# Score maxima of two attention heads taken in pairs, in two row groups of the matrix engine

## The chip, the cores and the metric

The kernel runs on one core of one Trainium2 chip. The metric is the device time of one execution in microseconds (us). Five engines work side by side, each with a queue of its own: PE (TensorE, the matrix engine), DVE (VectorE), ACT (ScalarE), POOL (GpSimd) and SP (SyncE, which issues most transfers). They meet at semaphores.

## The reference

One transformer layer in float32: causal attention over 4 sequences of 2048 tokens with 4 heads of 64, a residual and a layer norm, then a routed feed-forward part with 32 experts and 16 adapters, another residual and a layer norm.

```python
q = split_heads(x @ wq.T) * hd ** -0.25
k = split_heads(x @ wk.T) * hd ** -0.25
v = split_heads(x @ wv.T)
q, k = (_rope(q), _rope(k))
energy = jnp.einsum('bhtd,bhld->bhtl', q, k) + mask
attn = jax.nn.softmax(energy, axis=-1)
out = jnp.einsum('bhtl,bhld->bhtd', attn, v)
```

The change is in the attention stage alone. The softmax needs a shift for each query row that is near that row's largest score; which one exactly does not alter the result.

## The kernel before

**Tiles and stages.** `attention` works on pairs of heads, f = 0 to 7 (4 sequences, two pairs each). A sequence has 16 tiles of 128 tokens; four tiles of queries make a group, y = 0 to 31, with G = 0 to 3 its place in the sequence. A group of queries meets 4G + 4 tiles of keys. Group and head make a unit, u = 2y + head. Routing, experts and the last norm follow after the attention stage and are left as they are.

**Two passes over the scores.** First, for the maxima, PE multiplies one tile of queries (i) by up to four tiles of keys (c), with the scores in the layout queries x keys (`score`, L505 to L530). On the diagonal block (c == G) only (i + 1) tiles of keys take part, and a second small product adds the causal mask. DVE takes the maximum of each such entry (L796), and at the end of a unit the negative maximum of all entries (L801). A row step then turns the maxima into a row by four transposes (L515), and ACT copies that row into row 64 of `q_low` (L683). Second, for the values, PE computes the scores again, transposed, chunk by chunk (`ahead`, L532 to L549): L545 multiplies `k_st` (the rounded keys in rows 0 to 63, their rests in rows 64 to 127) with the rounded queries `q_two` (both halves alike), and L546 adds `k_one` (the rounded keys and a row of ones) times `q_low` (the rests of the queries and the row of negative maxima). ACT takes the exponential (L674). Every fourth chunk, PE multiplies four chunks of probabilities with the values (`multiply`, L562), 64 columns for each head.

**Slots.** All engines walk through the same list of slots, one for each of the 640 chunks (chunks of the two heads alternate) and some more (`walk`, L375). In slot g PE does the score entries that the planner put there, then a value batch if g % 4 == 3, then chunk g + 2, and then the late steps of the slot (projections, turning queries and keys, sums, the rows after the attention). `Plan` places the entries backwards from the slot six before their group begins, one a slot (L154 to L161), pushes them back where queries or keys come later (L180 to L189) and lets a row step follow two slots after the last entry of its unit.

**Banks.** The scores for the maxima go to two banks of `x_ps` in turn: entry e waits until entry e - 2 has been read (L509 to L511).

**Keys.** For a new tile of keys ACT copies the turned keys to `k_st` (L655), DVE puts the rests into its lower half (L766) and POOL copies the rounded half to `k_one` (L907). The ones are filled in by DVE: L752 for the first 12 places and L781 for the other 12.

**Totals.** DVE and POOL add up the probabilities of a group over its chunks (L370; DVE the odd ones, POOL the even ones). PE sums over the partitions by `pick` (L594, 8 products into 8 rows), DVE takes reciprocals (L833), PE spreads them over the 128 rows by `spread` (L601), and DVE scales the output (L829).

## Time and profile before

| | us |
|---|---|
| median of 3 runs | 2308.29 (2306.02 to 2310.01) |
| the profiled execution | 2305.32 |
| its span, first to last instruction | 2303.5 |
| first and last chunk product L546 | 63.0 and 1444.5 |

Mean granted clock of PE over the span: 0.897 of full speed.

| busy over the whole span | us | share |
|---|---|---|
| PE, matrix products | 1910.4 | 83% |
| PE, loads of weights | 1421.0 | 62% |
| DVE | 1589.0 | 69% |
| ACT | 1141.5 | 50% |
| POOL | 1388.5 | 60% |

How to read it: instructions are named by line, engine and operation, and by what is written from what. PE's products overlap in the records and their ends are modelled, so the distance between two starts says more than a duration. An engine's idle time is put down to the instruction whose semaphore ended it. Many shares are averages over stages that have different limits.

### The profile page before, as it was taken

Reading aid. Unit: us, or ns where it says so; the run is one execution under the profiler, and the core shown is the slowest. Engines: PE = TensorE matmul, PEld = TensorE weight load, DVE = VectorE, ACT = ScalarE, POOL = GpSimd, SP = SyncE. Lnnn points to the kernel's source line nnn. Section 1 sums busy time; section 2 is a strip of 40 time slices with the busy share of each in tenths; the row PEclk is TensorE's granted clock in tenths of the full one; section 3 lists DMA queues with packets and bytes.
Section 4 is the critical chain, followed back from the end, with each engine's and each line's share of the span. In section 5 each row is a group of like instructions: output and inputs, shape, how many; then the busy total and the mean of one; then the engine's idle time right before and its main releaser. Section 6 shows DMA issues by size and latency. Waiting matters only on the chain. (4 is left out here: it accounts for less than half of the span.)

```text
span 2303.5 us, 37026 instructions
## 1 busy us (share of the span) xinstructions
PE 1910.4 (83%) x10914; PEld 1421.0 (62%) x10914; DVE 1589.0 (69%) x3363; ACT 1141.5 (50%) x2709; POOL 1388.5 (60%) x1723
## 2 busy tenths in 40 slices
PE   5899998998998898998998998452277999999990
PEld 4555655655655555655655554351176999999980
DVE  8576776787777777787777775356794665566555
ACT  3344455455455444455444444224264666666655
POOL 3368777677777676777777644210075676667652
PEclk7799999999999999999999999555588999999995
DMA  2000011111011111011111011130003435554428
GB/s 76 7 12 17 22 40 33 38 42 33 21 35 35 38 38 37 17 40 33 42 35 38 8 42 49 36 140 1 0 1 122 137 129 160 164 153 139 148 53 292
DMA packets 100610, 144.06 MB, mean 63 GB/s; under 512 B 17956, under 2 KB 88592, under 8 KB 96364
## 3 DMA queue, kind: packets, MB, share of 16 engines
q1 hardware_dynamic: 84588, 132.04, 16.7%
q0 software_dynamic: 15872, 10.24, 2.7%
q8 instruction: 67, 1.10, 0.2%
q14 instruction: 83, 0.68, 0.1%
HBM read 113.14 MB, written 39.85 MB: 66 GB/s over the span
## 5 line engine op out<-in xcount | busy, mean ns | idle before, releaser
L674 ACT ACTIVATE probs<-scores_t_ps 128x512 f32<-128x512 f32 (+3 forms) x640 | 339.6, 533 | 495.7 <-PE scores_t_ps L546 295.7
L796 DVE TENSOR_REDUCE part_max<-scores_ps 128x1 f32<-128x512 f32 (+3 forms) x640 | 372.6, 599 | 87.8 <-PE scores_ps L526 52.9
L370 POOL TENSOR_TENSOR sums<-sums,probs 128x512 f32<-128x512 f32 (+3 forms) x288 | 328.2, 1139 | 19.0 <-ACT probs L674 13.4
L526 PE MATMUL scores_ps<-k_st,q_two 128*128 128x512 f32 (+3 forms) x640 | 273.7, 446 | 68.9 <-DVE q_low L821 31.3
L1571 PE MATMUL up_ps<-xe_t,w 128*128 128x320 f32 x1920 | 289.7, 311 | 1.7 <-DVE xe_t L1678 1.7
L562 PE MATMUL out_ps<-probs,v_sb 128*64 128x512 f32 (+3 forms) x1280 | 287.1, 568 | 0.2 <-ACT probs L674 0.2
L1571 PEld LDWEIGHTS up_ps<-xe_t,w 128*128 128x128 f32 x1920 | 284.9, 190 | 1.9 <-issue 1.9
L545 PE MATMUL scores_t_ps<-q_two,k_st 128*128 128x512 f32 (+3 forms) x640 | 274.1, 428 | 8.3 <-ACT probs L674 8.1
L370 DVE TENSOR_TENSOR sums<-sums,probs 128x512 f32<-128x512 f32 (+3 forms) x288 | 257.9, 896 | 2.2
L546 PE MATMUL scores_t_ps<-q_low,k_one 65*128 65x512 f32 (+3 forms) x640 | 239.5, 374 | 0.0
L1534 POOL DMA_INDIRECT acc_rows<-out_rows,token x96 | 148.7, 1549 | 127.5 <-ACT out_rows L1661 116.5
L526 PEld LDWEIGHTS scores_ps<-k_st,q_two 128*128 128x128 f32 x640 | 125.8, 201 | 133.4 <-DVE part_max L796 62.4
L1692 DVE SCALAR_TENSOR_TENSOR h<-silu,up_ps 128x320 f32<-128x320 f32 x160 | 77.1, 482 | 183.0 <-ACT silu L1648 183.0
L545 PEld LDWEIGHTS scores_t_ps<-q_two,k_st 128*128 128x128 f32 x640 | 125.6, 196 | 125.2 <-issue 110.7
L1571 PE MATMUL y_ps<-w,h_parts 128*128 128x256 f32 x1440 | 181.2, 285 | 0.0
L1571 PEld LDWEIGHTS y_ps<-w,h_parts 128*128 128x128 f32 x1440 | 174.7, 192 | 2.2
L1514 POOL DMA_INDIRECT rows<-x_rows,token_in x96 | 128.9, 1342 | 48.0 <-POOL token_in L1511 28.4
L562 PEld LDWEIGHTS out_ps<-probs,v_sb 128*64 128x64 f32 x1280 | 82.8, 143 | 121.1 <-issue 105.7
L1673 DVE TENSOR_TENSOR w<-w_raw,w 128x768 fp32r<-128x768 f32 x160 | 153.0, 958 | 5.0 <-ACT w L1626 1.2
L949 POOL TENSOR_TENSOR x<-powers_of,power 128x2 f32<-128x2 f32 x64 | 54.3, 849 | 151.9 <-DVE powers_of L867 151.9
L959 POOL TENSOR_TENSOR products<-qk,cos_sin 128x256 f32<-128x256 f32 x116 | 88.1, 760 | 92.4 <-ACT qk L646 69.9
L1626 ACT CAST w<-w_raw 128x768 fp32r<-128x768 f32 x160 | 131.7, 825 | 7.4 <-PEq L992 7.4
(317 smaller groups left out, 3941.4 us busy)
## 6 DMA issues: line engine op xcount, KB each, us to landing
w_raw<-in_w_expert SPq DMA_DIRECT2D x32, 1536.0 KB, 6.5
x_t<-in_x_t SPq DMA_DIRECT2D x128, 128.0 KB, 2.0
w_raw<-in_w_adapter SPq DMA_DIRECT2D x32, 384.0 KB, 7.2
x_row<-in_x SPq DMA_DIRECT2D x64, 128.0 KB, 2.0
x_rows<-x SPq DMA_DIRECT2D x64, 128.0 KB, 2.0
acc_rows<-x SPq DMA_DIRECT2D x64, 128.0 KB, 2.0
ln_x<-acc_rows SPq DMA_DIRECT2D x16, 512.0 KB, 6.1
out_rows_dram<-ln_y SPq DMA_DIRECT2D x16, 512.0 KB, 5.2
```

Source lines behind the costliest of these rows:

```text
L370: eng.tensor_tensor(side, side, probs[:, g % P_RING, i * P:CH], ALU.add).then_inc(summed[u % 2], 1)
L526: mm = pe.matmul(out[:, 0:n], q_two[:, ring, hh, cols(i)], k_st[:, hh, places(f * NT + 4 * c, 4)][:, 0:n], start=True, stop=not diagonal)
L545: pe.matmul(out, k_st[:, hh, places(f * NT + kb)], q_two[:, ring, hh, i * P:CH], start=True, stop=False)
L546: mm = pe.matmul(out, k_one[:, hh, places(f * NT + kb)], q_low[:, ring, hh, i * P:CH], start=False, stop=not diagonal)
L562: mm = pe.matmul(o_ps[hh * HD:(hh + 1) * HD, i * P:CH], v_sb[:, place(f * NT + kb), hh, :], probs[:, g % P_RING, i * P:CH], start=kb == 0, ...
L674: act.activation(probs[:, g % P_RING, i * P:CH], s_ps[:, g % 2, i * P:CH], ACT.Exp).then_inc(exp_done, 1)
L796: dve.tensor_reduce(part_max[:, u % 4, i, c:c + 1], x_ps[:, e % 2, 0:n], AX.X, ALU.max).then_inc(score_read, 1)
L1514: pool.indirect_dma_start(out=rows[0:n, r, t, :], out_offset=None, in_=dram["x1"], in_offset=bass.IndirectOffsetOnAxis(ap=token_in[0:n, r, ...
L1534: pool.indirect_dma_start(out=dram["acc"], out_offset=bass.IndirectOffsetOnAxis(ap=token[0:n, r, t:t + 1], axis=0), in_=out[0:n, r, t, :], ...
L1571: mm = pe.matmul(o, left(a), right(b), start=start and n == 0, stop=stop and n == 2)
L1626: act.copy(columns(w[:, r, 0], p), columns(w_raw[:, r], p)).then_inc(w_upper, 1)
L1673: dve.tensor_tensor(columns(w[:, r, 1], p), columns(w_raw[:, r], p), columns(raw(w[:, r, 0]), p), ALU.subtract).then_inc(w_split, 1)
```

## The change

The maxima of both heads are computed from the rounded queries and keys only, 64 rows deep, as a pair: head 0 in rows 0 to 63 of the array, head 1 in rows 64 to 127, into the two banks of `x_ps` at once. An entry is now one of a group y, not of a unit; the planner wants one every second slot, counted back from an even one, and never two in a slot. DVE takes both maxima in one reduction, and the row step turns both heads' maxima. Each entry waits for the one ahead of it to be read, since it fills both banks. `k_one` and `q_low` keep head 1 in their upper half with the row of ones or maxima in row 0, so that the product L546 of head 1 is 128 rows deep (zeros between), that of head 0 65 as before. ACT instead of POOL makes the second copy of the keys. The sums of the two heads go to rows 0 and 32 (two column groups), and the spread reads them from there in two row and two column groups. Shapes of buffers change accordingly.

```diff
@@ Plan
-        for u in reversed(range(len(self.units))):
-            G = self.groups[self.units[u][0]][1]
+        for y in reversed(range(len(self.groups))):
+            G = self.groups[y][1]
             for c in reversed(range(G + 1)):
                 for i in reversed(range(4)):
-                    cur = min(cur - 1, begin[u // 2] - 6)
-                    entries.append([cur, u, c, i])
+                    cur = min(cur - 2, begin[y] - 6)
+                    entries.append([cur, y, c, i])
...
-            s = max(wanted, at)
-            if u >= 4:
+            s = max(wanted, at + 1 if at >= 0 else at)
+            if y >= 2:
                 s = max(s, q_from[y])
             s = max(s, turned.get(f * NT + 4 * c + 3, -100) + 1)
-            while s >= 0 and s < begin[y] - 6 and taken.get(s, 0) >= 2:
-                s += 1
-            taken[s] = taken.get(s, 0) + 1
...
@@ PE, score
-                if e >= 2:
-                    kind, count = plan.emptied[e - 2]
+                if e >= 1:
+                    kind, count = plan.emptied[e - 1]
                     pe.wait_ge(row_read if kind == "row" else score_read, count)
                 if c is None:
-                    pe.wait_ge(neg_ready, u + 1)
+                    pe.wait_ge(neg_ready, y + 1)
                     for t in range(4):
-                        mm = pe.transpose(out[0:HD + 1, cols(t)], neg_pad[:, u % 2, t, :], ident[:])
+                        pe.transpose(x_ps[0:HD + 1, 0, cols(t)], neg_pad[:, y % 2, t, 0:HD + 1], ident[:])
+                        mm = pe.transpose(x_ps[0:1, 1, cols(t)], neg_pad[:, y % 2, t, HD + 1:HD + 2], ident[:])
...
-                    pe.wait_ge(k_lower, latest + 1)
+                    pe.wait_ge(k_again, latest + 1)
                 n = (i + 1) * P if diagonal else CH
-                mm = pe.matmul(out[:, 0:n], q_two[:, ring, hh, cols(i)], k_st[:, hh, places(f * NT + 4 * c, 4)][:, 0:n],
-                               start=True, stop=not diagonal)
+                for hh in range(2):
+                    half = slice(hh * HD, (hh + 1) * HD)
+                    mm = pe.matmul(x_ps[:, hh, 0:n], q_two[half, ring, hh, cols(i)],
+                                   k_one[half, hh, places(f * NT + 4 * c, 4)][:, 0:n], start=True, stop=not diagonal)
                 if diagonal:
-                    mm = pe.matmul(out[:, n - P:n], ident_b[:], causal[:], start=False, stop=True)
+                    for hh in range(2):
+                        mm = pe.matmul(x_ps[:, hh, n - P:n], ident_b[:], causal[:], start=False, stop=True)
@@ PE, sum and spread
-                        for i in range(4):
-                            n = 4 * hh + i
-                            mm = pe.matmul(out[0:8, 0:P], pick[:, n, :], sums[:, k % 2, hh, cols(i)],
-                                           start=n == 0, stop=n == 7)
+                    for i in range(4):
+                        for hh in range(2):
+                            mm = pe.matmul(out[32 * hh:32 * hh + 32, 0:P], pick[:, i, :], sums[:, k % 2, hh, cols(i)],
+                                           start=i == 0, stop=i == 3)
...
-                        mm = pe.matmul(out[:, cols(i)], spread[0:8, i].rearrange("p a b -> p (a b)"), inverse[:],
-                                       start=True, stop=True)
+                        for hh in range(2):
+                            row = slice(32 * hh, 32 * hh + 4)
+                            mm = pe.matmul(out[hh * HD:(hh + 1) * HD, cols(i)], spread[row, i, :], inverse[row, :],
+                                           start=True, stop=True)
@@ ACT
+                act.wait_ge(k_upper, n + 1)
+                act.copy(k_one[0:HD, 0, places(n)], k_st[0:HD, 0, places(n)])
+                act.copy(k_one[HD:P, 1, places(n)], k_st[0:HD, 1, places(n)]).then_inc(k_again, 1)
...
-                    act.copy(q_low[HD:HD + 1, ring, hh, :], x_ps[HD:HD + 1, e % 2, :]).then_inc(row_read, 1)
+                    act.copy(q_low[HD:HD + 1, ring, 0, :], x_ps[HD:HD + 1, 0, :])
+                    act.copy(q_low[0:1, ring, 1, :], x_ps[0:1, 1, :]).then_inc(row_read, 1)
@@ DVE
-            dve.memset(raw(k_one[HD:HD + 1, :, 0:FIRST * P]), 1.0)
+            dve.memset(raw(k_one[HD:HD + 1, 0, 0:FIRST * P]), 1.0)
+            dve.memset(raw(k_one[0:HD, 1, 0:FIRST * P]), 0.0)
+            dve.drain()
+            dve.memset(raw(k_one[0:1, 1, 0:FIRST * P]), 1.0)
...
-                dve.tensor_reduce(part_max[:, u % 4, i, c:c + 1], x_ps[:, e % 2, 0:n], AX.X, ALU.max).then_inc(score_read, 1)
+                dve.tensor_reduce(part_max[:, y % 2, :, i, c], x_ps[:, :, 0:n], AX.X, ALU.max).then_inc(score_read, 1)
@@ POOL
-            def again_k(n):
-                pool.wait_ge(k_upper, n + 1)
-                pool.tensor_copy(k_one[0:HD, :, places(n)], k_st[0:HD, :, places(n)])\
-                    .then_inc(k_again, 1)
```

## Rows read from the trace of the kernel before

**Rows 1.** Uses of tile k_one: durations (min/median/max, ns), first and last start, us
```profile
L546 PE MATMUL scores_t_ps<-q_low,k_one x640: 272/394/632, 63.0 to 1444.5; 65*128 65x512 f32 x128, 65*128 65x256 f32 x32
```
**Rows 2.** A stretch: us, busy of PE, PEld, DVE, ACT, POOL, clock, DMA, GB/s
```profile
900.00:1000.00 100.00, 93.88 (x522) 59.65 (x521) 75.50 (x146) 46.51 (x122) 74.22 (x106) 1.00 0.08 23
```
**Rows 3.** PE's timeline: start us, duration us, line, out<-in, shapes
```profile
300.31 0.50 PE L526 MATMUL scores_ps<-k_st,q_two 128*128 128x512 f32 x1
300.65 0.39 PE L545 MATMUL scores_t_ps<-q_two,k_st 128*128 128x512 f32 x1
...
310.81 0.40 PE L526 MATMUL scores_ps<-k_st,q_two 128*128 128x512 f32 x1
311.04 0.40 PE L545 MATMUL scores_t_ps<-q_two,k_st 128*128 128x512 f32 x1
311.27 0.40 PE L546 MATMUL scores_t_ps<-q_low,k_one 65*128 65x512 f32 x1
```
**Rows 4.** PE's timeline around sums, spread and statistics
```profile
610.68 0.40 PE L546 MATMUL scores_t_ps<-q_low,k_one 65*128 65x512 f32 x1
611.01 1.92 PE L594 MATMUL misc_b_ps<-sums,pick 128*8 128x128 f32 x16
612.85 0.50 PE L526 MATMUL scores_ps<-k_st,q_two 128*128 128x512 f32 x1
...
616.62 1.15 PE L601 MATMUL misc_a_ps<-inverse,spread 8*128 8x128 f32 x8
617.71 0.65 PE L515 MATMUL scores_ps<-ident,neg_pad 128*65 128x128 f32 x4
...
653.63 0.62 PE L457 MATMUL misc_b_ps<-x_ts,w_r1s 6*128 6x256 f32 x3
654.17 1.07 PE L457 MATMUL misc_a_ps<-w_o,attn_t 128*128 128x256 f32 x4
```
**Rows 5.** PE's timeline at a value batch
```profile
704.72 1.94 PE L562 MATMUL out_ps<-probs,v_sb 128*64 128x512 f32 x8
706.59 0.50 PE L545 MATMUL scores_t_ps<-q_two,k_st 128*128 128x512 f32 x1
706.93 0.40 PE L546 MATMUL scores_t_ps<-q_low,k_one 65*128 65x512 f32 x1
```
**Rows 6.** PE's timeline at diagonal entries
```profile
718.91 0.36 PE L526 MATMUL scores_ps<-k_st,q_two 128*128 128x256 f32 x1
...
719.16 0.48 PE L545 MATMUL scores_t_ps<-q_two,k_st 128*128 128x512 f32 x1
719.48 0.40 PE L546 MATMUL scores_t_ps<-q_low,k_one 65*128 65x512 f32 x1
...
720.98 0.49 PE L526 MATMUL scores_ps<-k_st,q_two 128*128 128x512 f32 x1
...
721.36 0.48 PE L545 MATMUL scores_t_ps<-q_two,k_st 128*128 128x512 f32 x1
```
**Rows 7.** DVE by shape, 100 to 1440 us: count | busy us, mean ns | idle before
```profile
L796 DVE TENSOR_REDUCE part_max<-scores_ps 128x1 f32<-128x512 f32 x428 | 283.2, 678 | 52.8 <-PE scores_ps L526 48.4 <-PE scores_ps L529 0.6 <-issue 0.2
L796 DVE TENSOR_REDUCE part_max<-scores_ps 128x1 f32<-128x256 f32 x60 | 24.8, 414 | 5.7 <-PE scores_ps L529 5.7
```
**Rows 8.** Line L526: what ended PE's idle time before it (us, times)
```profile
  DVE part_max L796: 84.5, 180
  ACT q_low L683: 32.0, 57
```
**Rows 9.** DVE's timeline at the start; [idle before, released by]
```profile
2.19 2.62 DVE L752 MEMSET k_one<- 1x3072 f32 x1 [0.68 <-issue]
5.16 0.96 DVE L756 CAST w_qkv<-attn 128x1536 fp32r<-128x1536 f32 x1 [0.35 <-DMA attn<-in_w_qkv]
```
**Rows 10.** POOL's copies of keys (tile k_one); an ACT copy by shape
```profile
L907 POOL CAST k_one<-k_st x128: 386/392/1194, 15.6 to 1312.3; 64x256 fp32r<-64x256 f32 x128
...
L649 ACT COPY v_sb<-misc_a_ps 128x128 f32<-128x128 f32 x95 | 25.8, 272 | 0.0
```

More of the change, by code:

```diff
@@ L178, in __init__ @@
         self.entries, self.last_entry, self.row_entry = [], {}, {}
-        rows, at, placed, taken = [], -100, [], {}
-        for wanted, u, c, i in entries:
-            y = self.units[u][0]
-            f = self.groups[y][0]
-            s = max(wanted, at)
-            if u >= 4:
+        rows, at, placed = [], -100, []
+        for wanted, y, c, i in entries:
+            f, G = self.groups[y]
+            s = max(wanted, at + 1 if at >= 0 else at)
+            if y >= 2:
                 s = max(s, q_from[y])
@@ L209, in __init__ @@
             (self.before if s < 0 else self.score_at[s]).append(e)
-        assert all(self.row_entry[u - 2] < self.last_entry[u] for u in range(2, len(self.units)))
+        assert all(self.row_entry[y - 2] < self.last_entry[y] for y in range(2, len(self.groups)))
         for m, (at, turn, last) in enumerate(post):
@@ L384, in walk @@
             turned(0, 4)
-            early_units = [e for e in plan.before if plan.entries[e][0] < 2]
+            early_units = [e for e in plan.before if plan.entries[e][0] < 1]
             for e in early_units:
@@ L535, in ahead @@
                 if kb == 0:
[L536 removed]
+                    pe.wait_ge(row_read, u // 2 + 1)
                 if f * NT + kb >= ones_seen[0]:
@@ L545, in ahead @@
                 pe.matmul(out, k_st[:, hh, places(f * NT + kb)], q_two[:, ring, hh, i * P:CH], start=True, stop=False)
-                mm = pe.matmul(out, k_one[:, hh, places(f * NT + kb)], q_low[:, ring, hh, i * P:CH], start=False, stop=not diagonal)
+                rows = one_rows(hh)
+                mm = pe.matmul(out, k_one[rows, hh, places(f * NT + kb)], q_low[rows, ring, hh, i * P:CH],
+                               start=False, stop=not diagonal)
                 if diagonal:
@@ L789, in score @@
             def score(e):
-                u, c, i = plan.entries[e]
-                f, G, hh, ring = unit(u)
+                y, c, i = plan.entries[e]
+                G = groups[y][1]
                 if c is None:
@@ L832, in step @@
                     dve.wait_ge(totals_ready, k + 1)
-                    dve.reciprocal(inverse[:], bank("sum", k)[0:8, 0:P]).then_inc(totals_read, 1)
+                    dve.reciprocal(inverse[:], bank("sum", k)[0:HD, 0:P]).then_inc(totals_read, 1)
                 elif kind == "ot_read":
```

101 lines of the change are left out of this document (51 added, 50 removed).

## The prediction

> **What bounds the kernel now.** I read the busy shares of the stretches first, then TensorE's (PE's) own timeline inside the attention stage, then who waits for whom on the lines of the change. The change touches only the attention stage, whose 640 chunk slots lie between 63 and 1444.5 us [rows 1], 2.16 us a slot. In a typical 100 us of it PE is busy 94%, VectorE (DVE) 76%, GpSimd (POOL) 74% and ScalarE (ACT) 47%, at a granted clock of 1.00, the 2.4 GHz level [rows 2]. So PE is the first candidate, but its busy share is made of modelled ends. What counts is the distance between the starts of two PE instructions. At full clock a column takes 0.417 ns, so 512 columns need 0.213 us; a 512-column product whose weights were loaded beside its predecessor is followed after 0.23 us (310.81 to 311.04), one whose weights were not after 0.34 us (300.31 to 300.65) [rows 3]. The 0.11 us between them is an exposed weight load, and the reader will meet it in every step below.
>
> Three rows show what a change of PE's array shape costs. The chunk product of 610.68 would be followed after 0.23 us, but the sums, eight columns wide, start after 0.33: entry 0.10. Their 16 steps of 128 columns, two passes each, need 16 x 0.107 = 1.71 us of columns, some 1.74 with what lies between two steps, and the next full-width product starts after 1.84: exit about 0.10. The statistics, six rows deep, run three products of 256 columns (0.107 each, 0.32) in 0.54 us: 0.11 for the first weights, 0.10 for the way out [rows 4]. And behind a value batch, which is 64 columns wide, the chunk product at 706.59 takes 0.34 us instead of 0.23: its weights are exposed too [rows 5]. An excursion into another shape therefore costs about 0.10 + 0.11 + 0.10, and 0.11 more behind it.
>
> **Maxima on PE.** The 640 products of L526 (one head, 128 rows) become 320 pairs (both heads, 64 rows each, in the lower and upper half of the array). From the groups' sizes (4, 8, 12, 16 tiles, eight times) 192 pairs lie off the diagonal and 128 on it. No row shows two row groups running at once. The nearest is the value batch: eight records of 512 columns, two passes each (0.427 us), start within one row of 1.94 us, which is four times 0.427 plus load and way out, not eight: two column groups run side by side with their own weights [rows 5]. I take the same for row groups; the ends are full overlap (one stream of 0.213) and none (two).
> Off the diagonal, before, over two slots: two products, 0.29 each (between 0.23 and 0.34, both frequent), and two chunk products behind them, 0.23 each (311.04 to 311.27): 1.04 us [rows 3]. After: entry 0.10, weights 0.11, one stream 0.21, exit 0.10, the chunk product behind it 0.34 [rows 4, 5], and in the slot without a pair a chunk product of 0.28 (again the middle): 1.14. So +0.10 x 192 = **+19 us**.
> On the diagonal, before: a 256-column product with its causal one takes 0.25 (718.91 to 719.16), a 512-column one 0.38 (720.98 to 721.36), so 0.285 on the mean over 128 to 512, and the chunk product behind 0.32 [rows 6]; two of both 1.21. After: 0.10 + 0.11 + 0.13 + 0.10, two causal products at full width 0.14 with their load, then 0.32 and 0.28: 1.18. -0.03 x 128 = **-4 us**.
> The halved streaming alone (0.21 x 192 + 0.13 x 128 = 57 us) is thus given back by the excursions. The Trainium skill, page "TensorEngine Tiling (Array Packing)", section Theoretical Speedup, promises up to twice the speed for a contraction of 64 or less, and its section Key Properties says that a change of tiling mode drains the engine. By the first alone this term would be -57 us; the rows on the sums and on the statistics agree with the second and put about 0.10 us on each side of it.
>
> **Sums and spread on PE.** The totals of the two heads (L594) go to two column groups instead of eight columns of one. Before 16 steps in 1.74 us; after, if the heads pair as in the value batch, 8: half of it, -0.87 us x 32 groups = **-28 us** [rows 4, 5]. Bounds: 0 if they don't pair. The spread (L601) takes 1.09 us now (616.62 to 617.71) [rows 4]; it becomes twice as many products in two row and two column groups, which pair back to the same: **0**, at most +0.89 x 32 = +28 us if they don't.
>
> **Waits of PE on the maxima.** PE sat 84.5 us before L526 for reductions and 32.0 for the row copies [rows 8]. A pair fills both banks, so it waits for the previous pair's reduction, and the double buffer is gone. One reduction of 1024 elements costs, by the slope of 256 to 512 elements (414 to 678 ns, 1.03 ns each) [rows 7], 150 + 1055 = 1.21 us, against 1.36 for two. Working the planner's rule through, 194 pairs stand two slots (4.3 us) behind their predecessor, which is ample, and 96 stand one slot behind it, where starts are pushed late by the queries or keys; 26 of those share a slot with a value batch, which hides the wait. 70 remain exposed. The row step (eight transposes, as many as two single ones) now has two ACT copies behind it before a pair may start; in 11 of 32 groups that pair is next in the same slot, in the others slots later, where 57 short waits stood. I take **0** for all waits, between -35 and +35 (rivals).
>
> **Around the start.** The constants of the keys grow from one 3072-element fill of 2.62 us to three of half that [rows 9], so 1.31 us more, and there are two such fills. The first has 0.35 us of slack before the weights land [rows 9], so +0.96; the second stands ahead of the first chunk: +1.31. The 12 pairs ahead of the first chunks alternate strictly between PE and DVE, losing at least load and stream, 0.32 us, each: +4. Together **+6 us**.
>
> **Keys' second copy.** POOL loses 128 copies (median 0.39 us); ACT gains two copies of 64 x 128 for each, near the 128x128 copy of 272 ns [rows 10], and a wait on its own first copy. That is some 0.55 us of ACT, 128 times, 70 us on an engine that is half idle. Queued behind it on ACT are the exponential of that slot and the next query copy, and PE waits for those two slots later. Mostly hidden; I take **+6**, between 0 and +20. What POOL and DVE win (128 x 0.39 us of POOL; 320 x 0.15 of DVE) is off the path: **-3**, between -20 and 0. The wider rests of the queries, the taller reciprocal and the 1-column transposes change no free size: 0.
>
> Sum: +19 - 4 - 28 + 0 + 0 + 6 + 6 - 3 = **-4 us**. The profiled execution took 2305.3 us (span 2303.5 and 1.8 around it), 3 us under the median of 2308.3; so 2301 for it, **2304 us** as a median.
>
> **Rivals.**
> Faster, waits fall away: the pairs two slots apart find their banks always free, and 40% of the 84.5 us [rows 8] goes: -34, 2270 us. For it: 194 of 290 pairs. Against it: the waits now stand mostly where entries are dense, and those stay dense.
> Slower, lock-step: where pairs stand one slot apart, PE may not stream the next while DVE reduces this one. DVE has 0.76 x 2.16 = 1.64 us of work in a slot, about 1.0 besides a reduction of 0.68 [rows 1, 2, 7]; with 1.21 it needs 2.2, and the hand-over (load and stream, 0.32, and the notice) comes on top instead of beside it. At 0.5 us for the 70 exposed pairs +35: 2339 us. It decides as soon as DVE's queue reaches a reduction later than a slot after its pair.
> Slower, the row groups don't run as said: if the second head's weights load only after the first's, 0.107 x 320 = +34 us, 2338; with no overlap +57, 2361. For it: no row of this trace; against it: the column groups of the value batch.
> Slower, the spread: both heads' products leave two row groups for one bank; if these take turns, 0.89 x 32 = +28 us, 2332. The Trainium skill, page "TensorEngine Tiling (Array Packing)", section Restrictions and Gotchas, says that different row tiles cannot use one PSUM bank at the same time. By that rule this rival holds; no row here shows it, since no products of the kernel before leave two row groups.
>
> **How the numbers follow.** Forecast 0.47, its own range 2290 to 2318; waits fall away 0.18; lock-step 0.15; row groups 0.11; spread 0.09. About 0.2% (4.6 us, 2303.7 to 2312.9) is what a measurement of this kernel tells from no change. Of the forecast's 0.47 some 0.23 lies below that, 0.14 inside, 0.10 above. Faster 0.23 + 0.18 = 0.41, same 0.14, slower 0.10 + 0.35 = 0.45. Both signs hold much, so the range reaches 2274 to 2345, leaving out the better half of the first rival and the worse half of the third.
>
> **What would show it.** Right: the two products of a pair start within 0.02 us, 0.21 us of stream and about 0.10 before and behind; the sums take 0.97 us instead of 1.84; the spread stays at 1.1; the chunk product behind a pair takes 0.34. Wrong: pair starts 0.11 or 0.21 apart; a spread near 2 us; PE's idle time before L526 for reductions far from 84.5. A lower granted clock in the attention stage, from a PE with more holes, would break the sum as a whole.

## The result and the profile after

The kernel after takes 2321 us (median of 17 runs, 2310.5 to 2328.4) beside 2306 us (17 runs, 2298.6 to 2314.7) for the kernel before on the same chip: a ratio of 1.0063, 95% interval 1.0047 to 1.0080, so 15 us slower. The forecast was 4 us faster. The time lies inside the predicted range; its direction is wrong. In the three groups of experiments below, each on another chip, the kernel before had 2304, 2302 and 2300 us, so ratios are compared rather than medians. A trace is of one execution of a kernel, and what is read from it can differ by some us from the medians.

The page of the kernel after (busy us, share of the span, instructions; its span is 2325.9 us, its mean granted clock 0.878 where the kernel before had 0.897):

```profile
PE 1895.3 (81%) x11170; PEld 1367.0 (59%) x11170; DVE 1533.0 (66%) x3015; ACT 1214.3 (52%) x2965; POOL 1330.6 (57%) x1597
```

PE's steps are what the prediction said. PE's timeline after (start, duration, line, x products that the view has merged into the row):

```profile
299.68 0.40 PE L550 MATMUL scores_t_ps<-q_low,k_one 128*128 128x512 f32 x1
300.00 0.50 PE L528 MATMUL scores_ps<-k_one,q_two 64*128 64x512 f32 x2
300.44 0.50 PE L548 MATMUL scores_t_ps<-q_two,k_st 128*128 128x512 f32 x1
300.77 0.40 PE L550 MATMUL scores_t_ps<-q_low,k_one 65*128 65x512 f32 x1
301.01 0.40 PE L548 MATMUL scores_t_ps<-q_two,k_st 128*128 128x512 f32 x1
301.24 0.40 PE L550 MATMUL scores_t_ps<-q_low,k_one 128*128 128x512 f32 x1
301.65 1.07 PE L599 MATMUL misc_c_ps<-sums,pick 128*32 128x128 f32 x16
302.69 0.50 PE L528 MATMUL scores_ps<-k_one,q_two 64*128 64x512 f32 x2
...
307.83 1.09 PE L608 MATMUL misc_c_ps<-inverse,spread 4*64 4x128 f32 x16
308.85 0.49 PE L528 MATMUL scores_ps<-k_one,q_two 64*128 64x512 f32 x2
```

Both products of a pair stand in one row of 0.50 us; taken singly they start 3 to 4 ns apart, in every pair that ran at 2.4 GHz. The chunk product follows 0.44 us after that start: one stream, not two. It is entered 0.32 us after L550 (0.23 plus the 0.10 of [rows 4]), and the chunk product behind it takes 0.33 [rows 5]. The sums take 1.04 us instead of 1.84 [rows 4], the spread 1.02 instead of 1.09. The reduction of 1024 elements costs the 1.21 us that the slope of [rows 7] gave (line L813 by form):

```profile
L813 DVE TENSOR_REDUCE part_max<-scores_ps 128x2 f32<-128x1024 f32 x224 | 271.5, 1212 | 91.8 <-PE scores_ps L528 83.7 <-PE scores_ps L532 4.6
L813 DVE TENSOR_REDUCE part_max<-scores_ps 128x2 f32<-128x512 f32 x32 | 21.8, 683 | 15.2 <-PE scores_ps L532 15.1
```

What is not as predicted is PE's waiting, and its clock. The 84.5 and 32.0 us of [rows 8] are not PE's idle time alone: that view adds the idle time of the weight loads (PEld) to that of the products. What ended the idle time of the products alone (us, times), L526 before and then L528 after:

```profile
  DVE part_max L796: 22.0, 51
  ACT q_low L683: 10.0, 23
```
```profile
  DVE part_max L813: 55.3, 80
...
  ACT q_low L694: 17.4, 15
```

Of the 55.3 us, 31.6 stand before the 96 pairs that follow their predecessor one slot later, 13.7 before the 194 that follow it two slots later, and 10.0 at the start.

The stretch of [rows 2] in the kernel after, and then the chunk stretch, from the first chunk product of the first slot to the last one (us, busy of PE, PEld, DVE, ACT, POOL, clock, DMA, GB/s):

```profile
900.00:1000.00 100.00, 88.86 (x456) 52.99 (x455) 60.89 (x94) 48.07 (x130) 61.82 (x83) 0.86 0.07 22
89.70:1465.90 1376.20, 1232.83 (x6858) 745.33 (x6857) 944.77 (x1852) 727.70 (x1991) 899.65 (x1191) 0.93 0.10 32
```

The same stretch of chunks in the kernel before:

```profile
82.90:1444.40 1361.50, 1241.91 (x6610) 794.42 (x6609) 1000.07 (x2190) 661.56 (x1758) 954.18 (x1307) 0.96 0.10 32
```

The stretch begins 6.8 us later and lasts 14.7 us longer; what follows it is within 1 us. PE's idle time in it (length less busy) went from 120 to 143 us, as much as its waits on the reductions grew. The clock went from 0.96 to 0.93: in the trace's records of the granted clock, PE stands at 1.2 GHz in 42 pieces with 191 us together, where the kernel before has 23 with 102 us.

One run of pairs, one slot apart, shows how the two hang together. All engines of the kernel after, between two such pairs:

```profile
597.30 0.50 PE L528 MATMUL scores_ps<-k_one,q_two 64*128 64x512 f32 x2 [0.65 <-DVE part_max L813]
...
597.73 0.33 PE L548 MATMUL scores_t_ps<-q_two,k_st 128*128 128x128 f32 x1
...
597.85 1.23 DVE L813 TENSOR_REDUCE part_max<-scores_ps 128x2 f32<-128x1024 f32 x1
...
599.13 0.51 PE L528 MATMUL scores_ps<-k_one,q_two 64*128 64x512 f32 x2 [0.89 <-DVE part_max L813]
...
600.19 0.42 PE L453 MATMUL misc_a_ps<-w_qkv,x_t_parts 128*128 128x384 f32 x1
```

From pair to pair 1.83 us: 0.55 until the reduction starts, 1.23 for it, 0.05 back to PE. PE is idle for 0.89 of it, and for 0.65 before the first of the two. Just behind (600.6 us) the granted clock falls. The same run of slots (232 to 239; the plans put other entries into them) takes 17.84 us after and 15.01 before, each with its clock:

```profile
585.69:603.53 17.84, 14.67 (x68) 8.48 (x66) 11.03 (x13) 7.12 (x21) 10.31 (x15) 0.82 0.05 16
```
```profile
577.90:592.91 15.01, 13.30 (x73) 8.28 (x72) 11.82 (x22) 5.92 (x17) 11.99 (x18) 1.00 0.06 17
```

**Theory.** PE's own steps were priced right. The step "waits: 0" failed: with both banks given to one pair the double buffer is gone, PE and DVE run in lock-step (each waits for the other in turn) where pairs stand one slot apart, and the holes bring PE down to 1.2 GHz. **Rivals:** the row groups themselves (changes of shape, or the clock); the row steps beside pairs; the keys' copy on ACT; VectorE too busy anywhere.

### The profile page after: what moved, and what is told of

Same layout as the page of the kernel before. It is cut to its first block and busy times, and to the rows that moved or that the text cites. A ratio compares the mean times of both kernels' runs of the same rounds, so it can differ in the third digit from the quotient of the medians.

```text
span 2325.9 us, 37201 instructions
## 1 busy us (share of the span) xinstructions
PE 1895.3 (81%) x11170; PEld 1367.0 (59%) x11170; DVE 1533.0 (66%) x3015; ACT 1214.3 (52%) x2965; POOL 1330.6 (57%) x1597
## 5 line engine op out<-in xcount | busy, mean ns | idle before, releaser
L813 DVE TENSOR_REDUCE part_max<-scores_ps 128x2 f32<-128x1024 f32 (+2 forms) x320 | 337.2, 1054 | 142.4 <-PE scores_ps L528 83.7
L548 PE MATMUL scores_t_ps<-q_two,k_st 128*128 128x512 f32 (+3 forms) x640 | 294.7, 461 | 13.9 <-ACT probs L684 12.7
L567 PE MATMUL out_ps<-probs,v_sb 128*64 128x512 f32 (+3 forms) x1280 | 294.3, 582 | 0.2 <-ACT probs L684 0.2
L528 PE MATMUL scores_ps<-k_one,q_two 64*128 64x512 f32 (+3 forms) x640 | 158.8, 492 | 107.4 <-DVE part_max L813 55.3
L550 PE MATMUL scores_t_ps<-q_low,k_one 65*128 65x512 f32 (+7 forms) x640 | 243.1, 380 | 0.0
L366 DVE TENSOR_TENSOR sums<-sums,probs 128x512 f32<-128x512 f32 (+3 forms) x288 | 229.4, 796 | 3.2 <-issue 0.6
L528 PEld LDWEIGHTS scores_ps<-k_one,q_two 64*128 64x128 f32 x640 | 63.8, 195 | 184.8 <-DVE part_max L813 89.6
L453 PE MATMUL misc_a_ps<-w_qkv,x_t_parts 128*128 128x384 f32 x576 | 145.2, 395 | 1.1 <-DVE q_low L838 1.1
```

The lines of the kernel that those rows point to most:

```text
L366: eng.tensor_tensor(side, side, probs[:, g % P_RING, i * P:CH], ALU.add).then_inc(summed[u % 2], 1)
L453: mm = pe.matmul(out, parts_l(a), parts_r(b), start=start and n == 0, stop=stop and n == 2)
L528: mm = pe.matmul(x_ps[:, hh, 0:n], q_two[half, ring, hh, cols(i)], k_one[half, hh, places(f * NT + 4 * c, 4)][:, 0:n], start=True, stop=no ...
L548: pe.matmul(out, k_st[:, hh, places(f * NT + kb)], q_two[:, ring, hh, i * P:CH], start=True, stop=False)
L550: mm = pe.matmul(out, k_one[rows, hh, places(f * NT + kb)], q_low[rows, ring, hh, i * P:CH], start=False, stop=not diagonal)
L567: mm = pe.matmul(o_ps[hh * HD:(hh + 1) * HD, i * P:CH], v_sb[:, place(f * NT + kb), hh, :], probs[:, g % P_RING, i * P:CH], start=kb == 0, ...
```

## The experiments

All measured values in one table. Ratio: against the kernel before in the same group of runs, with its 95% interval. Clock: median over the timed runs of the mean granted clock. Low: pieces at 1.2 GHz and their us, in the chunk stretch of the profiled run. Waits: us that PE's products for the maxima waited on DVE's reductions, 100 to 1440 us of the profiled run. Low is of one execution: the spread of the clock over the 17 runs of the kernel after (0.876 to 0.887) comes, by an estimate, to some 50 us at 1.2 GHz.

| kernel | median us | ratio (interval) | clock | low | waits |
|---|---|---|---|---|---|
| before | 2300 to 2306 | 1 | 0.900 | 23, 102 | 21.0 |
| after | 2321.1 | 1.0063 (1.0047 to 1.0080) | 0.880 | 42, 191 | 45.3 |
| e1_sums_only | 2285.6 | 0.9919 (0.9905 to 0.9933) | 0.898 | 21, 109 | 22.2 |
| e2_pairs_full | 2316.0 | 1.0064 (1.0041 to 1.0087) | 0.890 | 25, 113 | 58.7 |
| e3_row_later | 2318.1 | 1.0051 (1.0033 to 1.0069) | 0.877 | 40, 201 | 45.4 |
| e6_early_row | 2339.1 | 1.0140 (1.0119 to 1.0162) | 0.872 | 40, 229 | 39.0 |
| e7_half_max | 2252.2 | 0.9791 (0.9766 to 0.9815) | 0.893 | 24, 109 | 15.8 |
| e8_sums_half_max | 2240.7 | 0.9737 (0.9715 to 0.9759) | 0.900 | 19, 82 | 11.9 |
| e9_full_half_max | 2243.4 | 0.9743 (0.9719 to 0.9767) | 0.902 | 18, 85 | 23.0 |
| e10_keys_act | 2270.5 | 0.9861 (0.9840 to 0.9881) | 0.899 | 20, 102 | 24.1 |
| e11_half_close | 2277.9 | 0.9901 (0.9875 to 0.9926) | 0.889 | 29, 133 | 25.3 |
| e12_half_apart | 2299.4 | 0.9984 (0.9966 to 1.0003) | 0.885 | 37, 157 | 37.8 |
| e13_odd_slots | 2361.8 | 1.0282 (1.0257 to 1.0306) | 0.878 | 42, 195 | 53.1 |
| e14_pool_back | 2286.0 | 0.9941 (0.9920 to 0.9962) | 0.899 | 24, 113 | 23.9 |

**e1_sums_only**: before, plus the change's sums and spread.

```diff
-                            mm = pe.matmul(out[0:8, 0:P], pick[:, n, :], sums[:, k % 2, hh, cols(i)],
+                            mm = pe.matmul(out[32 * hh:32 * hh + 32, 0:P], pick[:, i, :], sums[:, k % 2, hh, cols(i)],
...
```

> The kernel before, with the sums and the spread of the two heads in two column and row groups as in the change, and nothing else of it: the maxima stay as they were. Theory (PE's own distances between starts set the time; the prediction's term of -28 us is right, and in the kernel after it is hidden by the waits that the paired maxima bring): the sums go from 1.84 to about 1.04 us and the spread stays at 1.0 to 1.1, 32 times, so about -26 us: some 2280 us, a ratio of 0.989. Rival (PE was not the bound, what it wins is idle elsewhere): within 5 us of the kernel before. Rival (mode changes of the array are dearer than their rows, so that the sums in column groups bring little): between -10 and 0.

Measured: 0.9919, -19 us. The theory's direction, and PE is a bound; but 26 us of streams became 19. PE's idle time in the chunk stretch, over all lines, rose from 120 to 132 us: part of what PE won it waits for elsewhere.

**e2_pairs_full**: after, with the pair's products in full width, one after the other.

```diff
-                    pe.wait_ge(k_again, latest + 1)
+                    pe.wait_ge(k_lower, latest + 1)
...
-                    half = slice(hh * HD, (hh + 1) * HD)
-                    mm = pe.matmul(x_ps[:, hh, 0:n], q_two[half, ring, hh, cols(i)],
-                                   k_one[half, hh, places(f * NT + 4 * c, 4)][:, 0:n], start=True, stop=not diagonal)
+                    mm = pe.matmul(x_ps[:, hh, 0:n], q_two[:, ring, hh, cols(i)],
+                                   k_st[:, hh, places(f * NT + 4 * c, 4)][:, 0:n], start=True, stop=not diagonal)
```

> The kernel after, but the two products of a pair run one after the other in full width: 128 rows of the stacked keys against 128 rows of the queries (the zero rows of each head make the sums the same), so that no row group is used for the maxima. The plan, the banks, the waits and the reductions of 1024 elements are those of the kernel after. Theory (the schedule costs: one buffer in place of two, the row step beside a pair): by the rows a pair off the diagonal costs about 0.10 + 0.32 and 0.11 behind it in row groups, and 0.23 to 0.34 twice in full width, so about the same time as the kernel after, 2305 to 2325 us, with the same runs of pairs costing the same. Rival (the change of the array's shape 320 times, or a chip effect that goes with row groups, is what makes the kernel after slow): clearly faster than the kernel after, by 40 us and more (2280 or less).

Measured: 1.0064, the ratio of the kernel after. So row groups are not what makes the change slow, and the schedule without them costs as much. But the clock is not the same: 0.890 against 0.880, although PE waits longer here (58.7 against 45.3 us; its idle time in the chunk stretch is 156 us against 143). A pair off the diagonal that waits for nothing is cheaper here than in row groups, at 2.4 GHz; from the chunk product ahead of it to the second one behind it:

```profile
324.16 0.39 PE L549 MATMUL scores_t_ps<-q_low,k_one 128*128 128x512 f32 x1
324.39 0.63 PE L527 MATMUL scores_ps<-k_st,q_two 128*128 128x512 f32 x2
324.86 0.39 PE L547 MATMUL scores_t_ps<-q_two,k_st 128*128 128x512 f32 x1
325.08 0.39 PE L549 MATMUL scores_t_ps<-q_low,k_one 65*128 65x512 f32 x1
```

That is 0.92 us; in row groups it was 1.09 (299.68 to 300.77 above). Over all such places the medians are 0.93 (18 pairs) and 1.10 (16). Behind a wait full width is dearer (0.57 us from the pair to its chunk product instead of 0.47), so this is not the price of every pair. This kernel also shows the price of the clock by itself, since equal slots of it ran at both levels (slots 232 to 239, 392 to 399, 552 to 559, then slot 303 and slot 383):

```profile
587.09:603.18 16.09, 12.12 (x68) 7.86 (x66) 10.85 (x13) 7.12 (x21) 9.84 (x14) 1.00 0.06 17
936.90:955.60 18.70, 14.95 (x68) 10.51 (x66) 11.16 (x13) 7.12 (x21) 9.61 (x14) 0.82 0.05 15
1283.54:1299.70 16.16, 12.12 (x68) 7.85 (x66) 11.44 (x13) 7.12 (x21) 9.78 (x14) 1.00 0.03 8
733.56:743.19 9.63, 9.63 (x33) 6.08 (x30) 2.90 (x6) 1.81 (x5) 2.97 (x5) 0.51 0.05 14
916.02:921.40 5.38, 5.38 (x33) 3.49 (x31) 3.12 (x6) 1.51 (x4) 3.19 (x6) 1.00 0.10 29
```

The same work takes 16.1 or 18.7 us, and 5.38 or 9.63 us. In the first three rows 6.8 us at 1.2 GHz cost 2.6 us, in the last two 9.3 us cost 4.2.

**e3_row_later**: after, with the row step three slots behind the last pair.

```diff
-                rows.append((min(s + 2, begin[y] - 3), y))
+                rows.append((min(s + 3, begin[y] - 3), y))
```

> The kernel after, with the row step (the transposes of the maxima and their two copies on ACT) planned three slots after the last pair instead of two; the slots that hold a row step and a pair go from 12 to 4. Theory (a row step leaves both banks to ACT's two copies, and the pair behind it in the same slot waits for them: 11 such slots cost 13 us more than in the kernel before): 8 of 12 are gone, so about -9 us, 2312 us. Rival (the row step's waits are hidden, or the lower granted clock is a matter of its own): no difference, within 3 us of the kernel after.

Measured: 1.0051, within its interval of the kernel after; not the 9 us. PE's waits on ACT's row copies fell only from 17.4 to 14.1 us. The price that I had read from the 11 slots with row step and pair does not go away when they are parted.

**e6_early_row**: e3_row_later, with the projections of the first tiles planned earlier.

```diff
-                    base = per * (f - 1) + (14 + 5 * t if f == 1 else 8 + 6 * t)
+                    base = per * (f - 1) + (8 + 5 * t if f == 1 else 6 * t)
...
-                    base = per * (f - 1) + 54 + 4 * (t - 8)
+                    base = per * (f - 1) + 54 + 2 * (t - 8)
```

> The kernel after, with the row step three slots after the last pair and the projections of the first tiles of each half planned earlier (by 6 slots and more), so that queries and keys push the pairs together less: pairs that stand one slot behind their predecessor go from 96 to 54, and no row step shares a slot with a pair. Theory (runs of pairs one slot apart cost 26 us, row steps beside pairs 13 us): some 44% of the first and all of the second go, about -20 to -25 us: 2296 to 2301 us, and fewer falls of the granted clock. Rival (the waits are not the cause, the price lies in every pair): within 5 us of the kernel after. Rival (the earlier projections crowd PE elsewhere): slower than the kernel after.

Measured: 1.0140, 18 us slower than the kernel after. The last rival holds. PE now waits for POOL's halves of the inputs, which it hardly did before (lines of the projections, 100 to 1440 us):

```profile
L453 PE MATMUL misc_c_ps<-w_qkv,x_t_parts 128*128 128x384 f32 x126 | 28.7, 366 | 8.8 <-POOL x_t_parts L922 8.8
L453 PE MATMUL misc_b_ps<-w_qkv,x_t_parts 128*128 128x384 f32 x102 | 23.1, 365 | 8.9 <-POOL x_t_parts L922 8.9
```

The pairs stood further apart, but 229 us at 1.2 GHz outweighed it. It says nothing on lock-step, and a cleaner cut was needed: leave plan and PE alone and shorten what PE waits for.

**e7_half_max**: after, with reductions over half the columns.

```diff
-                dve.tensor_reduce(part_max[:, y % 2, :, i, c], x_ps[:, :, 0:n], AX.X, ALU.max).then_inc(score_read, 1)
+                dve.tensor_reduce(part_max[:, y % 2, :, i, c], x_ps[:, :, 0:n // 2], AX.X, ALU.max).then_inc(score_read, 1)
```

> The kernel after, but each reduction reads only the first half of a chunk's columns (it leaves out half of the candidates of each maximum), so that one takes about 0.68 us instead of 1.16 and the banks come back sooner; PE's instructions, their order and the plan are those of the kernel after. Theory (PE's waits for the reductions in runs of pairs cost their own length and let the clock fall to 1.2 GHz behind them): the 45 us of waits on reductions between 100 and 1440 us go to some 10, the stretches at 1.2 GHz between the first and the last chunk from 42 with 191 us to some 26 with 115, so -35 and about -35 more: 2250 us. Rival (products on half the array's rows lower the clock by themselves, waits or not): the waits go, the stretches at 1.2 GHz stay near 40, -35: 2285 us. Rival (the waits were slack that another engine's chain sets): within 10 us of the kernel after.

Measured: 2252 us, 24 pieces with 109 us at 1.2 GHz, waits of 15.8 us: close to the theory's three numbers. The profiled spans differ by 75.5 us, and the parts add up: PE's idle time in the chunk stretch 143 to 108 us (-35), 82 us less at 1.2 GHz (-35 at the price below), a start 4.6 us sooner. The price comes from its own equal slots (232 to 239, 392 to 399, 552 to 559):

```profile
556.33:569.98 13.65, 11.84 (x68) 6.91 (x67) 7.24 (x13) 7.12 (x21) 10.20 (x14) 1.00 0.06 19
893.19:908.31 15.12, 13.32 (x68) 7.93 (x66) 7.35 (x13) 7.11 (x21) 10.00 (x14) 0.89 0.06 17
1227.60:1242.73 15.13, 13.32 (x69) 7.86 (x67) 7.35 (x13) 7.12 (x21) 10.02 (x14) 0.89 0.03 9
```

Here 3.4 us at 1.2 GHz cost 1.47 us, 0.43 for each us (0.38 and 0.46 in e2_pairs_full). In the kernel after this run of slots took 17.84 us: 4.2 more than 13.65. Its 6.4 us at 1.2 GHz make 2.7 of them at that price, which leaves 1.5 for its longer waits; PE's idle time there is 1.4 us longer.

**e8_sums_half_max** and **e9_full_half_max**: the same edit on e1_sums_only and on e2_pairs_full.

> The kernel before with sums and spread in two column groups, and with each single reduction over the first half of its columns (it leaves out half of the candidates), 0.41 us instead of 0.68: the control for the kernel after with halved reductions. PE's waits on reductions are 22 us between 100 and 1440 us and some 60 in all here, the stretches at 1.2 GHz are 21. Theory (two buffers had hidden most of the reductions already): -10 to -25 us against the same kernel with whole reductions, 2260 to 2275 us, with as many stretches at 1.2 GHz. Against this kernel the paired maxima with halved reductions are dearer by the prediction's +15 us, if the price of the row groups' steps was right.

> The kernel after with the products of a pair one after the other in full width and with each reduction over the first half of its columns (it leaves out half of the candidates of each maximum). Beside the same with row groups it gives the price of the row groups where no reduction is waited for. Theory (row groups cost about what two full-width products cost, and the waits do the rest): within 10 us of the kernel with row groups and halved reductions. Rival (row groups lower the clock by themselves): this one is faster than that one by 20 us and more, with fewer stretches at 1.2 GHz. Other rival (row groups save PE's streams at no price of their own): slower than that one by 10 to 40 us.

Measured: 0.9737 and 0.9743. The kernel with single maxima gains 42 us from halved reductions too, more than the 10 to 25 expected: even with two buffers VectorE's time counts. The paired one gains 63 (1.0063 to 0.9791); the 21 us between are the pairs' own. Where the reductions are short, full width beats row groups by 11 us (0.9743 to 0.9791, good to some 8 us), between the expectations: it has 85 us at 1.2 GHz instead of 109 (24 x 0.43 = 10 us), although PE waits longer in it (23.0 against 15.8 us). So the second clue of e2_pairs_full repeats: row groups go with a lower granted clock at no longer waits. And with full width the waits lower the clock little: from e2_pairs_full to e9_full_half_max PE's idle time falls by 33 us and its time at 1.2 GHz by 27, from the kernel after to e7_half_max by 35 and 82.

**e10_keys_act** and **e14_pool_back**: e1_sums_only with the keys' second copy on ACT; then POOL's old copies again on top, into a spare tile.

```diff
@@ e10_keys_act, ACT (POOL's copy is taken out)
+                act.wait_ge(k_upper, n + 1)
+                act.copy(k_one[0:HD, 0, places(n)], k_st[0:HD, 0, places(n)])
+                act.copy(k_one[0:HD, 1, places(n)], k_st[0:HD, 1, places(n)]).then_inc(k_again, 1)
@@ e14_pool_back, POOL, beside that
+                pool.wait_ge(k_upper, n + 1)
+                pool.wait_ge(spared, n)
+                pool.tensor_copy(spare[:], k_st[0:HD, :, places(n)]).then_inc(spared, 1)
```

> The kernel before with sums and spread in two column groups, and with the keys' second copy made by ACT in two copies of 64 x 128 as in the kernel after, instead of one by POOL; the maxima stay as they were. Prediction's term: +6 us, between 0 and +20, against the same kernel with POOL's copy: 2291 us (2285 to 2305). Theory (ACT has room in the slots of the copies): +6 or less. Rival (the copies hold up the exponential behind them on ACT, and PE two slots later): +15 and more, with a wait of PE on ACT's exponentials that grows from 8 us.

> The kernel before with sums and spread in two column groups and the keys' second copy on ACT (2270 us), to which POOL's old copies are added again, into a spare tile that nothing reads: POOL's load is again that of the kernel before, ACT's that of the kernel after. Theory (POOL was late for what PE and ACT wait for, and the 0.39 us x 128 taken from it are the 14 us): back to about 2284 us. Rival (the copy itself is ready sooner on ACT, or the order on ACT changed for the better): stays at 2270 us.

Measured: 0.9861, 13 us faster than e1_sums_only where prediction and expectation had 0 to +20. Adding POOL's copies again gives 0.9941: the gain is gone, so it is POOL's relief, not ACT's copy. A part is seen in PE's waits for the input halves that POOL makes. e1_sums_only, e10_keys_act and e14_pool_back, 100 to 1440 us:

```profile
L457 PE MATMUL misc_a_ps<-w_qkv,x_t_parts 128*128 128x384 f32 x570 | 131.3, 368 | 3.2 <-POOL x_t_parts L908 3.2
```
```profile
L457 PE MATMUL misc_a_ps<-w_qkv,x_t_parts 128*128 128x384 f32 x570 | 131.1, 368 | 1.4 <-DVE q_low L826 0.5 <-POOL x_t_parts L911 0.4
```
```profile
L459 PE MATMUL misc_a_ps<-w_qkv,x_t_parts 128*128 128x384 f32 x570 | 131.2, 368 | 3.8 <-POOL x_t_parts L915 3.3 <-DVE q_low L830 0.5
```

PE's idle time in the chunk stretch, over all lines, goes 132, 124, 134 us along with them. But POOL's copies also lengthen DVE's work. DVE's additions of the probabilities in the same three kernels, over the whole span:

```profile
L370 DVE TENSOR_TENSOR sums<-sums,probs 128x512 f32<-128x512 f32 (+3 forms) x288 | 256.2, 890 | 2.2
```
```profile
L370 DVE TENSOR_TENSOR sums<-sums,probs 128x512 f32<-128x512 f32 (+3 forms) x288 | 217.0, 753 | 2.2
```
```profile
L372 DVE TENSOR_TENSOR sums<-sums,probs 128x512 f32<-128x512 f32 (+3 forms) x288 | 252.1, 875 | 2.2
```

DVE is busy 1587, 1539 and 1581 us in all. So the gain may come by POOL's own lateness or by DVE's: PE's waits on POOL's input halves go 5.0, 1.1, 5.0 us over the chunk stretch, those on DVE's outputs `attn_t` 10.2, 5.0, 8.0. DVE's 48 us would be worth 14 by the 0.3 us for each that e8_sums_half_max shows, an estimate; no run parts the two ways. e10_keys_act, with the kernel before's maxima and the change's two other parts, is the fastest whole kernel here: 1.4% under the kernel before, 2.0% under the kernel after.

**e11_half_close** and **e12_half_apart**: after, with halved reductions only where the next pair stands one slot behind, or only where it doesn't.

```diff
+        pairs = [(s, e) for s in range(slots) for e in self.score_at[s] if self.entries[e][1] is not None]
+        self.close = {e for (s, e), (t, _) in zip(pairs, pairs[1:]) if t - s <= 1}
+        self.apart = {e for _, e in pairs} - self.close
...
+                if e in plan.close:
+                    n //= 2
```

> The kernel after, with the reductions over half the columns only for the 96 pairs that the next pair follows one slot later (half of the candidates of these maxima are left out); the 212 others in the slots stay whole. With all halved it ran 69 us faster, and the kernel before with column-group sums 43 us faster for the same. Theory (the loss of the second buffer bites where pairs stand one slot apart): these 96 bring 25 to 35 us of the 69, 2286 to 2296 us, and take most of the waits on reductions and most of the added stretches at 1.2 GHz with them (42 to about 28). Rival (VectorE is simply too busy, wherever the reductions stand): 96 x 0.5 us of 308 such savings, a good quarter of 69, about -18, 2303 us, stretches at 1.2 GHz about 37.

> The counterpart: the reductions over half the columns only for the 212 pairs whose next pair stands two or more slots later (half of the candidates of these maxima are left out); those of the 96 in runs stay whole. Theory (two causes: in runs the lost buffer, elsewhere only VectorE's load, which cost the kernel before 43 us as well): some -30 us, 2290 us, with the waits on reductions in runs and the stretches at 1.2 GHz about as in the kernel after (42 falling to no fewer than 35). Rival (the loss stands in every pair): -45 and more, 2275 us, stretches at 1.2 GHz falling in the same measure.

Measured: 0.9901 and 0.9984, so 37 us for the 96 close pairs and 18 for the 212 others. The lines of the maxima (100 to 1440 us), e11_half_close and e12_half_apart:

```profile
L531 PE MATMUL scores_ps<-k_one,q_two 64*128 64x512 f32 (+1 forms) x612 | 149.7, 485 | 76.5 <-DVE q_low L843 32.0 <-DVE part_max L818 25.3 <-ACT q_low L697 17.4
```
```profile
L531 PE MATMUL scores_ps<-k_one,q_two 64*128 64x512 f32 (+2 forms) x614 | 150.4, 486 | 86.4 <-DVE part_max L818 37.8 <-DVE q_low L843 30.2 <-ACT q_low L697 17.4
```

DVE's reductions are 47 us shorter in the first (337.2 to 290.7) and 93 in the second (243.9): a us of DVE is worth 0.8 in the runs of pairs and 0.2 elsewhere. e8_sums_half_max, with two buffers, gives 42 for 145 (383.2 to 238.6), 0.3. The theory of lock-step in runs of close pairs holds; "too busy anywhere" has the smaller share.

**e13_odd_slots**: after, with the pairs one slot earlier.

```diff
-                    cur = min(cur - 2, begin[y] - 6)
+                    cur = min(cur - 2, begin[y] - 7)
```

> The kernel after, with the pairs planned one slot earlier, so in odd slots: every second of them then holds a value batch, and VectorE adds up probabilities in the same slots. Pairs one slot apart become 117 instead of 96, pairs in slots of value batches 115 instead of 26. Theory (what counts is how soon VectorE has reduced a pair, and in odd slots the reduction stands ahead of or behind 0.6 us of adding): slower than the kernel after by 5 to 25 us, with more stretches at 1.2 GHz. Rival (PE has 1.94 us of value products to go on with, which hide the reduction): faster by 10 to 20 us.

Measured: 1.0282, 50 us slower than the kernel after, twice the worst expected. The clock is no worse (195 us at 1.2 GHz); PE's idle time in the chunk stretch grows from 143 to 173 us, of which 13 are a new wait of the row steps:

```profile
L514 PE MATMUL scores_ps<-ident,neg_pad 128*65 128x128 f32 x120 | 28.2, 276 | 15.0 <-DVE neg_pad L818 13.6 <-DVE part_max L813 1.4
```

From one chunk's start to the next, a slot with a value batch and a pair takes 4.69 us on the mean here, one with a value batch alone 3.62 in the kernel after: 1.07 for the pair, where a pair costs 0.68 in the other slots of the kernel after (1.74 against 1.06). In slots that ran at 2.4 GHz throughout it is 0.61 and 0.70. So a value batch does not hide a pair. The profiled spans differ by 33 us, not by 50 (that of the kernel after was one of its slower runs); the 30 us of idle time are nearly all of it.

## Why the prediction was wrong, step by step

| step | predicted us | measured us | from |
|---|---|---|---|
| sums in two column groups | -28 | -19 | e1_sums_only |
| spread | 0 | 0 (1.02 for 1.09 us) | timeline after |
| keys' copy, POOL's and DVE's relief | +6, -3 | -13 | e10_keys_act |
| start | +6 | +7 (first slot's chunk product, 82.9 to 89.7) | windows |
| maxima on PE, with the start, where reductions are short | +21 | +26 | e7 against e8, less the keys' copy |
| waits, with what they do to the clock | 0 | +21 | e7 and after, against e8 and e1 |

Each measured term is a difference of ratios times 2304 us, good to some 5 to 10 us. They add up to -19 - 13 + 26 + 21 = +15, the result, by the way in which they are formed: the sum checks nothing, and it takes for granted that the keys' copy is worth the same in every kernel.

**The waits are the step that failed.** I took 0 for them and left lock-step as a rival at 0.15. The rival was the mechanism: its loop (0.55 until the reduction starts, 1.23, 0.05) is 1.83 us at the row above, and e11_half_close puts the larger part in the runs of close pairs. Its reckoning of +35 was of the right size: +21 here. The pairs two slots behind their predecessor did not have "ample" time either: 13.7 us of waits stand before them. I also counted 26 pairs as hidden by a value batch; e13_odd_slots speaks against that. And I misread [rows 8]: of its 84.5 us only 22.0 are idle time of PE's products, 62.4 are that of weight loads. The rival of waits that fall away could therefore not have been worth 34 us; the 22.0 grew to 55.3.

**The clock carried most of it in this kernel.** The last sentence of the prediction named it, and no number stood behind it. Beside the 22 us between the two profiled spans, 89 us more at 1.2 GHz make +38 at 0.43 (34 to 41 at 0.38 to 0.46), and PE's idle time in the chunk stretch rose from 120 to 143 us; by this account the change would have been faster without both, as the forecast's sign had it. The 17 runs of the kernel after say the same without a trace: at a mean clock of 0.876 one took 2328.4 us, at 0.887 another 2310.5, 1.8 us for each 0.001 on the line through all. The kernel before stands at 0.900. Two things go with a lower clock, each shown by an exchange: the waits (0.880 to 0.893 from after to e7_half_max), and the row groups (0.880 against 0.890 in e2_pairs_full, 0.893 against 0.902 in e9_full_half_max). What about a row group does it (fewer columns, the changes of shape around it, half of the rows) is not shown. The lost buffer costs time without the clock too: with full width the same difference (e9_full_half_max and e2_pairs_full, against e8 and e1) is +32 us instead of +21, and there it is nearly all waiting, 156 us of idle time instead of 120 in the kernel before, at 113 us of 1.2 GHz instead of 102. Set side by side in their traces, row groups have 13 and 15 us less idle time than full width and start 4 us sooner; the clock takes back 34 and 10 us at 0.43, and 1 and 7 us remain for PE's steps. So what row groups win is waiting, not steps, and they end level with full width and 11 us behind it.

**PE's steps** were right in size (0.32, 0.44, 0.33 us on the timeline), and the rival that row groups don't overlap is out. The term as a whole is near, +26 for +21, but in part by luck: e7_half_max has 27 us more at 1.2 GHz than e8_sums_half_max (109 and 82), which make 12 of the 26 at 0.43, and the prediction had put the clock at nothing. The Trainium skill, page "TensorEngine Tiling (Array Packing)", section Theoretical Speedup, promises up to twice the speed for a contraction of 64 or less, from which the prediction made an estimate of -57 us. The two products of a pair do share one stream here, but in the whole kernel nothing of the 57 us is left: row groups and full width have the same ratio, 1.0063 and 1.0064. At 2.4 GHz alone the term may have been too dear. From e10_keys_act to the kernel after the profiled spans grow by 55 us; start (8), PE's idle time (20), 89 us more at 1.2 GHz (38) and what follows the last chunk (3) make 69, which leaves about -14 for the steps. This is a remainder, not a measurement. Where nothing waits, at 2.4 GHz, a pair off the diagonal adds 0.63 us to its chunk products; the two single products of the kernel before add 0.49 by the median and 0.63 by the mean. That is 0 to +0.14 a pair, where the sum had +0.10.

**The spread** did not take turns. Its 16 products leave two row groups for one bank in 1.02 us; the rival was worth +28 and measured 0. The Trainium skill, page "TensorEngine Tiling (Array Packing)", section Restrictions and Gotchas, says that different row tiles cannot use one PSUM bank at the same time. This trace does not show them held apart (the two products of a step start 6 to 7 ns apart), at least where the two also write different column groups.

**The sums** were mis-sized: their stream fell by 0.80 us x 32 = 26 us as forecast within 2, but the kernel won 19, and PE's idle time elsewhere grew by 12 us (120 to 132).

**The keys' copy** had the wrong sign. I had put POOL's 128 x 0.39 us [rows 10] "off the path" at -3. e14_pool_back shows that they were not. Whether they held up PE through POOL or through DVE's additions, which are 39 us shorter without them, is open.

## What to carry to other kernels

Before two half-size results are merged into one that fills all buffers, write down the loop that is left (start to release, release to start) and compare it with the slot: a mean share of busy time says nothing about it, and the price stands where the work is dense. Price a hole on PE not by its length alone but with the slower clock that can follow it: here as much again with row groups (35 us of idle time, 35 of clock from after to e7_half_max), a third of it with full width (33 and 12 us from e2_pairs_full to e9_full_half_max). Before adding up a view's idle time, see which engine's it is. And try the parts of a change alone: two of three were worth 1.4% together, and the third, the one that gave the change its name, cost 2.0%.

## What was not expected of the hardware

- Equal work at the two clock levels is easy to find in one trace: the same slots took 13.65 and 15.12 us, 5.38 and 9.63 us. A us at 1.2 GHz cost 0.38 to 0.46 us here.
- Products on half the array's rows went with a lower mean clock than full-width ones in the same schedule, by 0.009 to 0.010, twice, though PE waited less in them. What about them does it is not shown.
- Products that leave two row groups and two column groups for one bank ran side by side (16 in 1.02 us, as 8 had taken 1.09).
- POOL, at 74% busy, for which PE was seen waiting only some 5 us, was worth 13 us when its 128 copies (64 us in e1_sums_only) were taken from it.
- Those copies made another engine slower: DVE's additions of 128 x 512 took 1088 ns on the mean with them, 887 without, and 1058 when they were put back.
